# Convolution and attention in one kernel: the first layer's matrix products as 32-row tiles alone, two slots taken in turn

## The reference

```python
# layer 0: 32 models of 16 channels, 64 hidden units each
shifts = [x] + [padded[:, :, r + 1:r + 1 + h, c + 1:c + 1 + w] for r, c in the eight neighbours]
perception = jnp.concatenate(shifts, axis=1)              # 9 * 512 channels
per_g = perception.reshape(b, M, 9 * C, h, w)             # model m takes 144 of them in a row
hdn = relu(einsum('bmchw,mdc->bmdhw', per_g, w1) + b1)
dx = einsum('bmdhw,mcd->bmchw', hdn, w2) + b2
x = x + dx
# layer 1: attention over 1024 pixels, 128 inner channels, 512 outer
theta, phi, g = projections of x
attn = softmax(einsum('bno,bom->bnm', theta, phi), axis=-1)
y = einsum('bnm,bmo->bno', attn, g)
z = batch_norm(w_w y + w_b)
out = z + x
```

## Time and profile before

| | |
|---|---|
| median of 3 runs | 1449.98 us (1449.78 to 1450.07) |
| the profiled execution | 1450.02 us, its span in the profile 1448.2 us |
| TensorE (PE) busy | 1431.0 us, 99% of the span |
| VectorE, ScalarE, GpSimd busy | 814.2, 738.0 and 255.9 us |
| granted TensorE clock | 1.0 of full speed but for the first slice |
| one batch (image) | 88.4 to 88.8 us from projection to projection |

### The profile page before, as it was taken

One profiled execution on the slowest core, in us unless ns is written; L12 is line 12 of the kernel. 1 busy time (PEld: TensorE's weight loads), 2 busy tenths in 40 slices (PEclk: granted clock), 3 DMA queues, 4 the chain that ended last, 5 costly groups with the idle time before them and its releaser, 6 DMA issues.

```text
span 1448.2 us, 27321 instructions
## 1 busy us (share of the span) xinstructions
PE 1431.0 (99%) x10364; PEld 796.4 (55%) x10364; DVE 814.2 (56%) x1033; ACT 738.0 (51%) x1175; POOL 255.9 (18%) x134
## 2 busy tenths in 40 slices
PE   7999999999999999999999999999999999999998
PEld 2454646546474564745546465464654646456477
DVE  1364665656646555565646556466564665656546
ACT  3464464644545554455543646446464454645544
POOL 0030220302213021130211203122030220302113
PEclk9999999999999999999999999999999999999999
DMA  4143543536435364263544534455343543536401
GB/s 137 65 156 136 189 167 123 175 118 219 155 119 188 111 217 146 107 214 118 185 146 143 200 136 146 146 179 177 123 175 117 208 153 119 180 111 233 151 30 59
DMA packets 129803, 216.31 MB, mean 149 GB/s; under 512 B 7328, under 2 KB 79008, under 8 KB 129696
## 3 DMA queue, kind: packets, MB, share of 16 engines
q1 hardware_dynamic: 129696, 214.62, 42.4%
HBM read 110.25 MB, written 104.33 MB: 148 GB/s over the span
## 4 chain that ended last, share of the span: by engine, by line
PE 98%; ACT 0%; DMA 0%; DVE 0%; issue 0%; SPq 0%; DVEq 0%
PE ps L444 32%; PE ps L460 8%; PE ps L477 8%; PE ps L499 6%; PE ps L500 6%; PE ps L504 6%; PE ps L534 4%; PE ps L521 4%; PE ps L522 4%; PE ps L523 4%; PE ps L541 4%; PE ps L538 4%; PE ps L553 2%; PE ps L554 2%; PE ps L558 2%; PE ps L618 1%
## 5 line engine op out<-in xcount | busy, mean ns | idle before, releaser
L444 PE MATMUL ps<-windows,w_main 64*64 64x512 f32 x4096 | 461.4, 596 | 8.2 <-DMA windows<-in_x 8.2
L716 ACT ACTIVATE hidden<-ps,columns 128x512 f32<-128x512 f32 x512 | 303.3, 702 | 321.4 <-PE ps L460 321.4
L1112 POOL TENSOR_TENSOR probs<-probs,row_inv 128x1024 f32<-128x1024 f32 x128 | 255.2, 1998 | 1175.0 <-DVE row_inv L908 1175.0
L444 PEld LDWEIGHTS ps<-windows,w_main 64*64 64x64 f32 x4096 | 151.6, 132 | 306.7 <-issue 306.7
L745 ACT ACTIVATE probs<-ps,neg_max 128x1024 f32<-128x1024 f32 x128 | 145.6, 1148 | 137.8 <-DVE neg_max L902 137.8
L913 DVE STREAM_TRANSPOSE probs<-probs 128x1024 f32<-128x1024 f32 x120 | 148.3, 1236 | 102.8 <-POOL probs L1112 102.8
L902 DVE TENSOR_REDUCE neg_max<-ps 128x1 f32<-128x1024 f32 x128 | 156.4, 1223 | 86.7 <-PE ps L523 78.5
L884 DVE SCALAR_TENSOR_TENSOR x1s<-ps,columns,windows 128x512 f32<-128x512 f32 x128 | 94.5, 745 | 125.8 <-PE ps L477 124.2
L922 DVE TENSOR_TENSOR x_lo<-x_lo,x_hi 128x1024 fp32r<-128x1024 f32 x120 | 141.8, 1213 | 23.9 <-ACT x_hi L752 23.9
L499 PE MATMUL ps<-x_hi,wp_hi 128*128 128x512 f32 x384 | 150.2, 391 | 1.8 <-issue 1.8
L500 PE MATMUL ps<-x_hi,wp_lo 128*128 128x512 f32 x384 | 149.5, 389 | 0.0
(11 more groups left out here) (78 smaller groups left out, 1358.2 us busy)
## 6 DMA issues: line engine op xcount, KB each, us to landing
rows_out<-probs SPq DMA_DIRECT2D x120, 512.0 KB, 3.1
x_lo<-rows_out SPq DMA_DIRECT2D x120, 512.0 KB, 4.8
out<-x1s SPq DMA_DIRECT2D x30, 1024.0 KB, 4.4
windows<-in_x SPq DMA_DIRECT2D x64, 298.0 KB, 4.8
windows<-in_x SPq DMA_DIRECT2D x64, 264.0 KB, 5.2
rows_out<-g_t SPq DMA_DIRECT2D x15, 512.0 KB, 2.6
g_raw<-rows_out SPq DMA_DIRECT2D x15, 512.0 KB, 6.1
out<-x1s SPq DMA_DIRECT2D x8, 256.0 KB, 2.1
```

The source lines that it names most:

```text
L444: product = mm(ps[HIDDEN * which:HIDDEN * (which + 1), hidden_bank(n, s, q), :], w_main[rows, p, which, :], shifted(windows[rows, chunk % ...
L716: activation(hidden[:, s % HIDDEN_HELD, q, :], ps[:, hidden_bank(n, s, q), :], ACT.Relu, bias=b1s[:, column:column + 1]).then_inc(hidden_r ...
L1112: nc.gpsimd.tensor_tensor(rows, rows, row_inv[:, e].to_broadcast([P, PIXELS]), ALU.mult).then_inc(normalized, 1)
```

## The change

For images 1 to 15 `mains` and `left` are replaced by `conv(n, s)`, which does slots s and s+1 together. All five units of a model are now separate products on 32 x 64 tiles, eight side by side; pair q uses row tile (q + step) % 4 at step 0 to 4, and the two slots take turns at each step, so that one's sums end while the other's run. A step of one slot is 8 products (16 instructions). The bank waits of both slots now stand ahead of their first step. Image 0 keeps `mains` and `left`.

With it come new bank tables and new orders on all engines: score row 3 is put ahead of the last projection (half 1 of g); on VectorE the transposes of rows, `split_y` and the sums stand in another order; on ScalarE `exp_row(n, 3)` comes before the last `bias_projection`, rows 4 to 7 are exponentiated in one go, and `round_y(n, 1)` comes behind the first `round_x1`. Score row 5's second half waits for relu 5 instead of relu 4 (`ROW_RELUS`).

```diff
-        SLOT_BANKS = [(6, 7, 4, 5), (0, 1, 2, 3), (4, 5, 0, 1), (2, 3, 6, 7),
-                      (2, 3, 6, 7), (1, 4, 5, 0), (5, 0, 2, 3), (6, 7, 1, 4)]
+        SLOT_BANKS = [(4, 5, 0, 7), (1, 6, 2, 3), (0, 1, 6, 7), (2, 3, 4, 5),
+                      (2, 3, 4, 5), (7, 0, 1, 6), (1, 4, 2, 3), (6, 5, 7, 0)]
-        DX_BANKS = [6, 7, 5, 0, 1, 4, 0, 2]
-        ROW_BANKS = [0, 2, 0, 2, 6, 4, 0, 2]
-        Y_BANKS = [4, 5]
-        Z_BANKS = [(2, 3, 6, 7), (3, 6, 7, 1)]
+        DX_BANKS = [4, 5, 1, 6, 7, 0, 4, 2]
+        ROW_BANKS = [0, 2, 0, 2, 4, 0, 6, 2]
+        ROW_RELUS = [(1, 2), (3, 5), (6, 6), (7, 8)]
+        Y_BANKS = [0, 1]
+        Z_BANKS = [(2, 3, 4, 5), (3, 6, 5, 7)]
...
+                elif s == 0 and q == 2 or s == 1 and q == 0:
+                    await_exp(n - 1, 2)
                 elif s == 0:
+                    await_ahead(tp_split, (n - 1) * 4 + split_step(1, PH) + 1)
+                elif s == 1 and q == 1:
                     await_ahead(proj_biased, (n - 1) * 6 + proj_step(1, G) + 1)
                 elif s == 1:
-                    await_exp(n - 1, 2 + q // 2)
+                    await_exp(n - 1, 3)
...
+            def conv(n, s):
+                awaited = set()
+                for unit_step in range(UNITS_READ):
+                    for turn in range(2):
+                        half, grp = divmod(s + turn, GROUPS)
...
+                        if unit_step == 0:
+                            for q in range(GROUP_PAIRS):
+                                await_bank(n, s + turn, q)
+                        else:
+                            await_ahead(units_summed[turn], ((n - 1) * 4 + s // 2) * 32 + 8 * unit_step)
+                        for q, which, tile, unit in places:
+                            p = GROUP_PAIRS * grp + q
+                            rows = slice(UNIT * tile, UNIT * (tile + 1))
+                            left_over = unit_step == (0 if p % 2 else 4)
+                            weights = w_left[rows, grp, which, :] if left_over else w_main[rows, p, which, :]
+                            product = mm(ps[HIDDEN * which:HIDDEN * (which + 1), hidden_bank(n, s + turn, q), :],
+                                         weights, shifted(windows[rows, unit % UNITS // 4, :], unit // UNITS, half),
+                                         start=(unit_step == 0), stop=(unit_step == UNITS_READ - 1),
+                                         skip_group_check=True)
+                            if unit_step < UNITS_READ - 1:
+                                product.then_inc(units_summed[turn], 1)
+                            elif which == SECOND:
+                                product.then_inc(hidden_summed, 1)
...
-                        pe.wait_ge(hidden_ready, (n + 1) * SLOT_PAIRS + 2 * (i - HALF_QBLOCKS) + half + 1)
+                        pe.wait_ge(hidden_ready, (n + 1) * SLOT_PAIRS + ROW_RELUS[i - HALF_QBLOCKS][half])
...
                 scores(n, 2)
+                scores(n, 3)
                 project(n, 1, G)
-                scores(n, 3)
-                mains(n + 1, 0)
-                mains(n + 1, 1)
-                left(n + 1, 0)
-                left(n + 1, 1)
+                conv(n + 1, 0)
```

More of the change, by code:

```diff
@@ L210, in conv_attention @@
         main_begun = sem("main_begun")
+        units_summed = [sem(f"units_summed_{h}") for h in range(2)]
         hidden_summed = sem("hidden_summed")
@@ L410, in await_bank @@
                     await_sum(n, q)
-                elif s == 6 and q < 2:
-                    await_hidden(n, 5, q + 2)
+                elif s == 6 and q == 0:
+                    await_hidden(n, 5, 2)
                 elif s == 6:
-                    await_out(n - 1, 0, q - 2)
-                elif q < 2:
-                    await_out(n - 1, 0, q + 2)
+                    await_out(n - 1, 0, (q + 1) % 3)
+                elif q == 0:
+                    await_hidden(n, 5, 3)
+                elif q == 1:
+                    await_out(n - 1, 0, 3)
@@ L417, in await_bank @@
                 else:
                     await_sum(n, q + 2)
+            def conv(n, s):
[3 more added lines that the diff above has]
+                        half, grp = divmod(s + turn, GROUPS)
+                        places = []
+                        for q in range(GROUP_PAIRS):
+                            for which in (FIRST, SECOND):
+                                unit = PAIR_UNITS * (GROUP_PAIRS * grp + q) + 4 * which + unit_step
+                                places.append((q, which, (q + unit_step) % 4, unit))
+                        for q, which, tile, unit in places:
+                            b = unit % UNITS // 4
+                            if (s + turn) % GROUPS == 0 and b not in awaited:
+                                awaited.add(b)
+                                await_ahead(top_loaded[b] if half == 0 else rest_loaded[b], (n + 1) * 16)
+                        if unit_step == 0:
+                            for q in range(GROUP_PAIRS):
+                                await_bank(n, s + turn, q)
+                        else:
+                            await_ahead(units_summed[turn], ((n - 1) * 4 + s // 2) * 32 + 8 * unit_step)
+                        for q, which, tile, unit in places:
+                            p = GROUP_PAIRS * grp + q
[10 more added lines that the diff above has]
+                                product.then_inc(hidden_summed, 1)
@@ L483, in project @@
                     pe.wait_ge(x1_rounded, n * SLOTS + GROUPS)
-                elif (half, w) == (0, PH) and first_image(n):
+                    pe.wait_ge(x1_ready, n * SLOTS + 7)
+                elif (half, w) == (0, PH) and not first_image(n):
+                    pe.wait_ge(out_added, (n - 1) * SLOTS + GROUPS + 2)
+                elif (half, w) == (0, G) and first_image(n):
                     pe.wait_ge(ww_split, 1)
-                elif (half, w) == (0, G) and not first_image(n):
-                    pe.wait_ge(out_added, (n - 1) * SLOTS + GROUPS + 3)
                 elif (half, w) == (1, PH):
@@ L579, in batch @@
                 dx(n + 1, 1)
-                mains(n + 1, 2)
-                mains(n + 1, 3)
-                left(n + 1, 2)
-                left(n + 1, 3)
+                conv(n + 1, 2)
                 attend(n, 0)
@@ L586, in batch @@
                 dx(n + 1, 3)
-                mains(n + 1, 4)
-                mains(n + 1, 5)
-                left(n + 1, 4)
-                left(n + 1, 5)
+                conv(n + 1, 4)
                 output(n, 0)
@@ L593, in batch @@
                 dx(n + 1, 5)
-                mains(n + 1, 6)
-                mains(n + 1, 7)
-                left(n + 1, 6)
-                left(n + 1, 7)
+                conv(n + 1, 6)
                 attend(n, 1)
@@ L680, in _ @@
             project(LAST, 0, G)
+            scores(LAST, 0)
             project(LAST, 1, TH)
-            scores(LAST, 0)
             scores(LAST, 1)
@@ L688, in _ @@
             scores(LAST, 3)
+            scores(LAST, 4)
             turn_row(1)
-            scores(LAST, 4)
             scores(LAST, 5)
             turn_row(2)
-            attend_turned(0)
-            turn_row(3)
             scores(LAST, 6)
             scores(LAST, 7)
+            turn_row(3)
+            attend_turned(0)
             turn_row(4)
@@ L1016, in batch @@
                 split_row(n, 7)
-                split_y(n, 1)
                 split_x1(n + 1, 1 - parity, 0)
                 split_x1(n + 1, 1 - parity, 1)
+                split_y(n, 1)
                 split_x1(n + 1, 1 - parity, 2)
                 sum_x1(n + 1, 1 - parity, 6)
+                add_out(n, parity, 1, 0)
                 split_x1(n + 1, 1 - parity, 3)
-                add_out(n, parity, 1, 0)
                 add_out(n, parity, 1, 1)
```

108 lines of the change are left out of this document (55 added, 53 removed).

## The result

The changed kernel takes 1508.85 us (median of 4 runs, 1504.39 to 1510.54), the kernel before 1450.03 in the same session (4 runs, 1449.78 to 1451.26): 1.0401 times as long, 95% interval 1.0389 to 1.0413. The forecast was 1462.5, with a range up to 1471. The direction was right, the time was 46 us off.

The account below looks back on a forecast made before the run. TensorE, holding 98% of the chain, was taken to bound the kernel. Losses 1.60 less gain 0.80 gave +0.80 a batch, +12.0 over 15 batches, +0.5 for the last image: 1450.0 + 12.5 = 1462.5 us, range 1446 to 1471.

Parts of the forecast that it names:

- the list of what costs nothing: Transposes, the rows' way out and back, `attend` and the waits between steps: all hidden, no loss counted.
- Late y, 0.31: Output product of half 1 waits for later y: 0.31 in 8 of 15 batches, hidden at the jump; 0.17 a batch.
- Block 2's stall, 0.48: Slots 2 and 3: slot 3's first product waits behind row 7's exponential and four awaits; 0.48 us, bounds 0.05 to 0.6.
- Block 1's stall, 0.36: Slots 0 and 1: second slot's first product waits for g's bias and stacked awaits; 0.36 us, bounds 0.05 to 0.45.
- Score row 5, 0.30: Row 5's second half waits for relu 5 instead of relu 4, with late weights: 0.30 us, bounds 0.15 to 0.35.
- Blocks 3 and 4: Second slots wait for banks of dx 3 and dx 5: stalls of 0.15 and 0.14 us.
- One shape change less, 0.17 a block: Each block keeps 20 steps but saves one tile-shape change: 0.17 us, 4 x 0.17 = 0.68 a batch gained.
- The waits between the steps: Waits on `units_summed` in each block, eight of them, said to be hidden by the other slot's turn: no cost.
- the rival: Step waits show in each block: 1486 us if each is 0.05 late, 1472 at 0.02; chance 8%.
- The 0.3 for eight increments: Step wait's passing time if eight increments double it: passes at 1.36 of 1.71, loads done at 1.62, just in time.
- The last image, +0.5: Its changed order puts waits in other places: an end 0.5 us later, bounds -2 to +1.5.
- +0.80: Net loss of each of 15 batches: losses of 1.60 us less a gain of 0.80.

Follow-up runs that it names:

- y_first: The changed kernel with y of half 1 rounded and split ahead of the next image's input again, as before the change: 1499.92 us, ratio 1.0347.
- orders_y_first: The changed kernel's banks and orders with the old `mains` and `left`, and y of half 1 rounded and split first: 1453.35 us, ratio 1.0020.
- after_unrolled: The changed kernel with TensorE's loop written out, the other engines keeping their loops: 1528.46 us, ratio 1.0513.
- after: The changed kernel itself, against the kernel before: 1508.85 us, ratio 1.0401.
- pad_16: The changed kernel with 16 always-true waits ahead of the odd images' first block: 1525.4 us, ratio 1.0535.
- half_conv: The changed kernel with the second model's product left out from the second step on; steps, waits and banks stay: 1478.12 us, ratio 1.0188.
- orders_only: The changed kernel's bank tables and orders, with the old `mains` and `left` in place of `conv`: 1471.2 us, ratio 1.0142.

## Why the prediction was wrong

- **The step that failed is the list of what costs nothing.** It held the engines' waits and banks against each other and said nothing of the instructions themselves. In `conv` a step of 0.43 us is 8 products and 8 loads; in `mains` it was 4 and 4. Pieces of code then came too late, in gaps of 0.8 to 3.9 us that cost 29 us. Shown by half as many products (gone), by 48 always-true waits (block 4 and `output(n, 0)` clean), by 16 (moved by 16 instructions), by the loop written out (sixteen gaps, all at the same place in a piece) and by the old products with the new orders (none). That the steps' waits (`units_summed`) add to it, by keeping the sequencer from running ahead of TensorE, is my reading and not shown.
- **Late y, 0.31, "in the seven batches that end the loop's body it hides".** The 0.31 is there (3.20 against 2.89). The hiding is the reverse of what happens: the jump begins only after the wait for y, so a late y is paid again there, 8.9 us in six jumps (the seventh branch isn't taken). Of the 59.7 us this is the second part that the list had at nothing; `y_first` and `orders_y_first` gave most of it back. I had the earlier trace rows and read its 0.33 as room, where it was the end of a chain that starts at that very wait.
- **Block 2's stall, 0.48**: 0.53 to 0.74 in the loop. The mechanism was right; two register instructions between the waits were allowed for in the bounds of block 1 and left out in block 2.
- **Block 1's stall, 0.36**: 0.28 to 0.32. **Score row 5, 0.30**: 0.30 for the four rows, and 0.24 of it is relu 5 by the two parts that I had added up, 0.13 and 0.11. What I missed is row 6's wait behind it, so that freeing row 5 alone gives back 0.08. **Blocks 3 and 4**: 8.95 to 9.02 and 8.93 to 8.99, where about 8.85 was said for both. Near enough.
- **One shape change less, 0.17 a block**: borne out. 20 steps of 0.429 are 8.59, and block 4 with its stall of 0.15 takes 8.94.
- **The waits between the steps**: the rival didn't occur. They pass 0.26 to 0.34 after their sums' end where four increments took 0.15, and each step is 0.43. The 0.3 for eight increments was my estimate, the time of four doubled, and lies within what the trace shows.
- **The last image, +0.5**: +1.1.

An undisturbed batch is 1.29 longer where +0.80 was said: with 19.3 for these and 1.1 for the last image, a kernel without late code and longer jumps would take about 1470, at the upper end of the range. The direction would have come out by that part alone; the size is code and jumps, 38 of the 59.7 us. What stays open: why a piece is asked for with none or some 40 instructions left in one place and over 100 in another, and so which ends of pieces show. The long gaps of images 11 and 13 are in the profile of one run and not in that of another with the same code at that place.

## What to carry to other kernels

Count the instructions of the engine that is the bottleneck, per microsecond, before and after a change. Where the same work takes twice as many, fetching code can be a cost (29 us here), and its place moves with every instruction added, so that a harmless edit costs or gains 1% (17 us with 16 always-true waits, 19 with 48). To tell such a gap from a wait, count instructions: here the gaps that were late code left the same remainder when their counts were divided by 256 (193 for all sixteen in `after_unrolled`). The jump began 0.17 us after y's split, the last thing that the loop's body waits for, in every looped kernel here: measure from there to the end of the body, and put that wait early. Writing the loop out takes the jumps away, but it gained 5 us for the kernel before and cost 20 for the changed one. And when a wait is taken out, look for the one that it had hidden.

## What the runs showed of the hardware

- Pieces of 16,384 bytes of code, 256 instructions each (counts in `after`, `after_unrolled`, `pad_16`; 30 pieces for 7680 instructions in `half_conv`); where one was late, products resumed 1.2 to 1.8 us behind its last packet, in gaps of 0.8 to 6.3 us.
- A taken branch on TensorE's sequencer: 3.3 to 3.9 us, begun 0.17 after the result that the last open wait was for, in every looped kernel here.
- Waits that are already true pass every 0.15 us (`after`: 267.91, 268.06, 268.21); a register instruction between two of them adds 0.09 to 0.18 there.
- After the gap of 3.6 us in image 11 the granted clock stood at 0.50 for 3.4 us (nine products 0.43 apart). After the jumps' gaps of 2.2 to 2.5 us in `orders_only` it fell to 0.50 in three of six cases.
